# A vision tower on one core: the combine weights stay on chip, the ring of expert weights gets four places, and half of the last residual moves to TensorE

## What is computed

```
h = einsum('bnk,dk->bnd', patches(x), W)                     # 64 x 196 tokens of 192
a = attention(h)       # 12 heads, silu on q, k, v, causal decay instead of a softmax, gate, Wo, layer norm
h = layernorm(h + a)
xn = rms_norm(h); logits = l2(slots) * scale . l2(xn)         # 64 slots
dispatch_w = softmax(logits, over tokens); combine_w = softmax(logits, over slots)
y = einsum('btd,bst->bsd', xn, dispatch_w)                   # the slots' inputs
y = gelu(y @ fc1[s] + b1[s]) @ fc2[s] + b2[s]                # each slot has its own expert: 192 -> 768 -> 192
h = layernorm(h + einsum('bsd,bst->btd', y, combine_w))
```

## Time and profile before

| | us |
|---|---|
| median of three runs | 1286.35 |
| the profiled execution's own time | 1285.4 |
| its span, first to last instruction | 1283.7 |
| TensorE busy with products | 1189.2 (93%) |
| VectorE busy | 816.2 (64%) |
| ScalarE busy | 735.8 (57%) |
| GpSimd busy | 571.7 (45%) |
| granted TensorE clock, mean over the span | 0.957 |

### The profile page before, as it was taken

The page is one execution under the profiler, slowest core; times in us unless marked ns, Lnnn a source line. Parts: engine busy times, 40 slices in busy tenths (PEclk is TensorE's granted clock), DMA queues, the critical chain, the costliest instruction groups (busy, mean ns, idle before and its releaser), DMA issues.

```text
span 1283.7 us, 34970 instructions
## 1 busy us (share of the span) xinstructions
PE 1189.2 (93%) x12938; PEld 956.2 (74%) x12938; DVE 816.2 (64%) x2114; ACT 735.8 (57%) x1677; POOL 571.7 (45%) x878
## 2 busy tenths in 40 slices
PE   5999999999999999999999999999998999997463
PEld 4788888888888888888888888888886555554232
DVE  4677676777777777767777777777673222222797
ACT  5456676776767666777767676666753111110566
POOL 3355455554555554545555455555433000000564
PEclk8999999999999999999999999999999999998555
DMA  4412111111111111111111111121071999994886
GB/s 142 187 49 74 66 53 59 51 50 50 50 50 50 50 66 72 53 54 55 50 50 50 50 50 50 56 81 53 14 265 68 385 419 422 419 393 100 229 261 187
DMA packets 50549, 158.34 MB, mean 123 GB/s; under 512 B 5338, under 2 KB 31312, under 8 KB 38096
## 3 DMA queue, kind: packets, MB, share of 16 engines
q1 hardware_dynamic: 32912, 145.04, 31.0%
q10 hardware_dynamic: 17600, 12.78, 3.2%
HBM read 132.18 MB, written 25.62 MB: 123 GB/s over the span
## 4 chain that ended last, share of the span: by engine, by line
PE 77%; DVE 16%; issue 2%; DMA 1%; ACT 1%; SPq 1%; DVEq 1%; POOL 0%; ACTq 0%; POOLq 0%
PE ps L933 11%; PE ps L934 10%; PE ps L935 10%; DVE p_sb L789 7%; PE ps L993 7%; PE ps L1028 6%; PE ps L1207 5%; PE ps L1224 4%; PE ps L1071 3%; PE ps L976 3%; PE ps L977 3%; PE ps L1011 2%; PE ps L1229 2%; PE ps L1238 2%; DVE res L902 2%; PE ps L1094 2%
## 5 line engine op out<-in xcount | busy, mean ns | idle before, releaser
L412 POOL TENSOR_TENSOR xl<-x_sb,xh 128x392 fp32r<-128x392 f32 x192 | 189.0, 1015 | 86.0 <-DVE gn L764 78.0
L789 DVE TENSOR_TENSOR p_sb<-ps,dec 98x1176 f32<-98x1176 f32 x128 | 176.9, 1382 | 56.0 <-PE ps L993 56.0
L993 PE MATMUL ps<-qm,kT 32*98 32x196 f32 x1536 | 117.0, 343 | 9.6 <-DVE p_sb L789 7.5
L644 ACT ACTIVATE hg<-ps 128x768 f32<-128x768 f32 x32 | 26.0, 812 | 157.2 <-PE ps L1229 157.2
L1028 PE MATMUL ps<-p_sb,vpad 98*32 98x98 f32 x3072 | 112.4, 250 | 1.9 <-DVE p_sb L789 1.9
L1028 PEld LDWEIGHTS ps<-p_sb,vpad 98*32 98x32 f32 x3072 | 84.5, 109 | 35.4 <-issue 24.7
L993 PEld LDWEIGHTS ps<-qm,kT 32*98 32x98 f32 x1536 | 75.2, 158 | 35.1 <-DVE p_sb L789 23.0
L894 DVE COPY y2st<-ps 128x192 f32<-128x192 f32 x32 | 11.4, 358 | 131.4 <-PE ps L1207 131.4
L1253 PE MATMUL ps<-y2b,cbuf 64*98 64x192 f32 x256 | 50.6, 549 | 43.9 <-POOL y2b L512 43.9
L661 ACT ACTIVATE o_sb<-res,nb,rstd 98x192 f32<-98x192 f32 x128 | 59.6, 536 | 51.8 <-DVE nb L917 51.2
L456 POOL TENSOR_TENSOR invn<-nrm,expo 98x4 f32<-98x4 f32 x32 | 32.7, 1021 | 117.7 <-DVE nrm L774 117.4
(11 more groups left out here) (186 smaller groups left out, 3640.9 us busy)
## 6 DMA issues: line engine op xcount, KB each, us to landing
x_sb<-in_xT SPq DMA_DIRECT2D x32, 1176.0 KB, 5.1
w1v<-in_fc SPq DMA_DIRECT2D x32, 1152.0 KB, 7.9
w2v<-in_fc SPq DMA_DIRECT2D x32, 1152.0 KB, 10.5
h_dram<-h SPq DMA_DIRECT2D x32, 294.0 KB
h2r<-h_dram SPq DMA_DIRECT2D x32, 294.0 KB
out<-o_sb ACTq DMA_DIRECT2D x32, 294.0 KB
comb_dram<-cst SPq DMA_DIRECT2D x32, 98.0 KB, 1.7
cbuf<-comb_dram SPq DMA_DIRECT2D x32, 98.0 KB, 3.9
```

Of the source, the lines that this page charges most:

```text
L412: pool.tensor_tensor(xl[:, k], x_sb[:, k], xh[:, k].bitcast(F32), ALU.subtract)\
L789: dve.tensor_tensor(dst, src, rate.unsqueeze(2).to_broadcast([T, PAIRS, 2, TOK]), ALU.mult)\
L993: mm = pe.matmul(ps[0:T, SC_AT + r, mt * TOK:(mt + 1) * TOK].rearrange("p (b n) -> p b n", b=2), kT[rows, g, n], qm[rows, g, :, n], start= ...
```

## The change

- The combine weights of all steps stay on chip in `comb` (25 KB of each partition). Their store, their load and the waits for both are gone.
- The ring of expert weights has four places, all loaded at the end of the first stage. The ring of outputs has four too.
- The two bias products of a pair stand next to each other, ahead of the first products of both halves.
- `y2r` has a place of its own. The rows of pairs 0 to 26 are loaded while the last pairs are computed; only those of pairs 27 to 31 come after the last store. The loads of the first `h2r` stand behind the early rows.
- After the second stage TensorE does 24 products of the identity with itself into a bank that nobody reads.
- In the third stage the residual of tiles 0 and 1 is added by TensorE: a product of the identity and `h2r` starts the bank, the combine products add to it. VectorE adds only tiles 2 and 3, takes the statistics of tiles 0 and 1 from PSUM, does `shift` of the step before, and then the statistics of tiles 2 and 3. ScalarE reads tiles 0 and 1 from PSUM. TensorE's steps of this stage are written out and not in a loop.

```diff
-RING = 6
-TURNS, REST = NU // RING, NU % RING
-assert RING % 2 == 0 and REST % 2 == 0
+RING = 4
...
+U_SOON = 27
+PARTS = ((0, 2 * DEEP), (2 * DEEP, NP))
+Y2 = RING
...
-        slot_at = [region_at + 4 * (2 * F + Y2 * D + n * SLOT) for n in range(EARLY)]
-        place = placer(slot_at[REST])
-        y2r = place("y2r", [128, NP, D])
-        place = placer(slot_at[EARLY - 1] + 4 * SLOT)
-        cbuf, h2r = place("cbuf", [128, DEEP, TOK]), place("h2r", [T, DEEP, 4, D])
-        place = placer(region_at + STAGE_AT)
-        y2b = place("y2b", [128, DEEP, D])
-        res, o_sb = place("res", [T, DEEP, 4, D]), place("o_sb", [T, DEEP, 4, D])
+        y2r, y2b = place("y2r", [128, NP, D]), place("y2b", [128, DEEP, D])
+        comb = place("comb", [128, NP, TOK])
+        place = placer(region_at + 4 * (2 * F + Y2 * D))
+        h2r, res, o_sb = place("h2r", [T, DEEP, 4, D]), place("res", [T, DEEP, 2, D]), place("o_sb", [T, DEEP, 4, D])
...
-            sp.wait_ge(k_mm, 2)
-            for n in range(EARLY, RING):
-                load_weights(n, n)
...
+            def load_y2(u0, u1, p0, p1, there):
+                for a in range(2):
+                    rows = slice(64 * a + 2 * u0, 64 * a + 2 * u1)
+                    sp.dma_start(y2r[rows, p0:p1, :], y2_dram[2 * u0:2 * u1, a, p0:p1, :]).then_inc(there, 16)
+
+            sp.wait_ge(fc2_mm, NU - 4)
+            for m in range(Y2):
+                sp.wait_ge(y2_stored[m], 16 * ((U_SOON - m + Y2 - 1) // Y2))
+            for p in range(0, NP, 2 * DEEP):
+                load_y2(0, U_SOON, p, p + 2 * DEEP, y2r_soon)
+            sp.wait_ge(fc2_mm, NU - 2)
             sp.wait_ge(h2_stored, 16 * NP)
-            sp.wait_ge(comb_stored, 16 * NP)
             for n in range(DEEP):
-                load_comb(n, n)
                 load_h2(n, n)
             for m in range(Y2):
                 sp.wait_ge(y2_stored[m], 16 * ((NU - m + Y2 - 1) // Y2))
             for (p0, p1), there in zip(PARTS, y2r_loaded):
-                for a in range(2):
-                    sp.dma_start(y2r[64 * a:64 * a + 64, p0:p1, :], y2_dram[:, a, p0:p1, :]).then_inc(there, 16)
+                load_y2(U_SOON, NU, p0, p1, there)
             with sp.Fori(0, NP // DEEP - 1) as w:
                 for n in range(DEEP):
                     p = DEEP * w + n
-                    sp.wait_ge(cmb_mm, p + 1)
-                    load_comb(p + DEEP, n)
-                    sp.wait_ge(res_rdy, p + 1)
+                    sp.wait_ge(mv3_rdy, 4 * p + 4)
                     load_h2(p + DEEP, n)
...
+            pool.wait_ge(y2r_soon, 32 * NP // (2 * DEEP))
             pool.wait_ge(y2r_loaded[0], 32)
...
-                    pool.wait_ge(cmb_mm, p + 1)
+                    pool.wait_ge(cmb_mm, 2 * p + 2)
                     bias(p + DEEP, n)
...
-                if d_before:
-                    act.wait_ge(comb_stored, 16 * j)
                 act.wait_ge(cb_mm, j + 1)
-                act.activation(cst[:, :], ps[:, 4, 0:TOK], ACT.Copy).then_inc(cb_sb, 1)
+                act.activation(comb[:, j], ps[:, 4, 0:TOK], ACT.Copy).then_inc(cb_sb, 1)
...
-                    act.activation(o_sb[:, n, t], res[:, n, t], ACT.Identity,
+                    src = ps[0:T, 2 * n, t * D:(t + 1) * D] if t < 2 else res[0:T, n, t - 2]
+                    act.activation(o_sb[:, n, t], src, ACT.Identity,
                                    bias=nb3[:, n, t:t + 1], scale=rstd3[:, n, t:t + 1]).then_inc(o_rdy, 1)
...
-                dve.wait_ge(cmb_mm, p + 1)
+                dve.wait_ge(cmb_mm, 2 * p + 1)
                 dve.wait_ge(h2r_loaded[n], 16 * w + 16)
                 if not at_start(w):
                     dve.wait_ge(o_rdy, 4 * (p + 1 - DEEP))
-                dve.tensor_tensor(res[0:T, n].rearrange("p (x t) d -> p x (t d)", x=2),
-                                  ps[0:T, 2 * n:2 * n + 2, 0:2 * D],
-                                  h2r[:, n].rearrange("p (x t) d -> p x (t d)", x=2), ALU.add)\
-                    .then_inc(res_rdy, 1)
+                dve.tensor_tensor(res[0:T, n].rearrange("p t d -> p (t d)"), ps[0:T, 2 * n + 1, 0:2 * D],
+                                  h2r[:, n, 2:4].rearrange("p t d -> p (t d)"), ALU.add).then_inc(res_rdy, 1)
+                dve.wait_ge(cmb_mm, 2 * p + 2)
+                for t in range(2):
+                    dve.bn_stats(st3[:, n, t, :], ps[0:T, 2 * n, t * D:(t + 1) * D])
+                if not (at_start(w) and n == 0):
+                    shift(p - 1, (n - 1) % DEEP)
                 dve.wait_ge(res_rdy, p + 1)
-                for t in range(4):
-                    dve.bn_stats(st3[:, n, t, :], res[0:T, n, t])
+                for t in range(2):
+                    dve.bn_stats(st3[:, n, 2 + t, :], res[0:T, n, t])
                 dve.drain()
                 for t in range(4):
                     dve.bn_aggr(mv3[:, n, t, :], st3[:, n, t, :]).then_inc(mv3_rdy, 1)
-                if not (at_start(w) and n == 0):
-                    shift(p - 1, (n - 1) % DEEP)
...
                     pe.matmul(ps[:, x, 0:FH], pickb[:, n % 2, x:x + 2].rearrange("p s b -> p (s b)"), bias1[:, f],
                               start=True, stop=False)
+                for x in range(2):
+                    f = slice(x * FH, (x + 1) * FH)
                     for s in range(2):
                         at = 64 * half_of(s, x)
                         pe.matmul(ps[at:at + 64, x, 0:FH], y_u[:, u, s], w1v[n][:, s, f], start=False, stop=False)
...
+            idle_products(6, 24)
             def out_step(p, n, w):
-                pe.wait_ge(cbuf_loaded[n], 16 * w + 16)
-                pe.wait_ge(y2b_rdy, p + 1)
                 if not at_start(w):
                     pe.wait_ge(res_rdy, p + 1 - DEEP)
-                for t in range(4):
+                pe.wait_ge(y2b_rdy, p + 1)
+                for t in (2, 3, 0, 1):
                     a, k = t // 2, t % 2
+                    if t == 0:
+                        if not at_start(w):
+                            pe.wait_ge(o_rdy, 4 * (p + 1 - DEEP))
+                        pe.wait_ge(h2r_loaded[n], 16 * w + 16)
+                        pe.matmul(ps[0:T, 2 * n, 0:2 * D], ident[0:T, 0:T],
+                                  h2r[:, n, 0:2].rearrange("p t d -> p (t d)"), start=True, stop=False)
                     mm = pe.matmul(ps[0:T, 2 * n + a, k * D:(k + 1) * D],
-                                   cbuf[64 * a:64 * a + 64, n, k * T:(k + 1) * T],
-                                   y2b[64 * a:64 * a + 64, n, :], start=True, stop=True)
-                mm.then_inc(cmb_mm, 1)
-            phase3(pe, out_step)
+                                   comb[64 * a:64 * a + 64, p, k * T:(k + 1) * T],
+                                   y2b[64 * a:64 * a + 64, n, :], start=(a == 1), stop=(t != 0))
+                    if k:
+                        mm.then_inc(cmb_mm, 1)
+            for p in range(NP):
+                out_step(p, p % DEEP, p // DEEP)
```

More of the change, by code:

```diff
@@ L266, in phase2 @@
                     step(RING * v + n, n, v)
-            for n in range(REST):
-                step(RING * TURNS + n, n, TURNS)
         def phase3(eng, step):
@@ L334, in _ @@
             store_h2(NP - 4)
-            store_comb(NP - 4)
             store_h2(NP - 3)
```

27 lines of the change are left out of this document (4 added, 23 removed).

## The result

The changed kernel takes 1291.87 us (median of six runs, 1290.67 to 1293.48) against 1286.37 for the kernel before on the same chip: 1.0039 times as long, interval 1.0027 to 1.0051. It is slower by 5.5 us, where 4.7 less had been forecast, and it lies above the top of the range, 1289.

The account below looks back on a forecast made before the run. TensorE was taken to bound the experts' stage, DMA nearly as full, and VectorE most of the third. Gains of 1.6 us (second stage) and 2.6 (third) made 4.2 off 1285.4, 1281.2; 1281.6 was forecast, range 1271 to 1289.

Parts of the forecast that it names:

- part 4: Slots' outputs loaded early, start of third stage: the 11.50 us wait gone, first combine product at T + 6.5.
- T: End of the last expert product, where the third stage starts; 1174.17 us in the kernel before.
- an early load that isn't early: Rival: the early load lands behind the end of stage two; up to 11.5 us back, 1291; chance 0.02.
- Part 1: Combine weights on chip without store or load, and two early weight loads gone: all costed at nothing.
- Part 2: Both bias products first, in the experts' stage: 0.18 us less a pair, bounds 0 and 0.25; 5.67 us a pair.
- The reading of the Trainium skill by which nothing is gained: Rival: the second bias product's weights wait for the first; pair stays 5.853 us, total 1283.5; chance 0.15.
- Part 3: Ring of four, experts' stage: DMA sets 5.81 us a pair, so 1.6 of the 5.6 us gain is kept.
- Part 5: The third stage's new step: 2.94 us against 2.66 before, 2.57 for the last three; TensorE's step 2.1 us.
- the circle: Third stage: `bn_aggr`, GpSimd's `rstd`, `shift` beside `y2b`, two statistics, next `bn_aggr`; 2.94 us a step.

Follow-up runs that it names:

- u24: The changed kernel with the early rows of 24 pairs in place of 27; 1288.39 us, ratio 1.0018 to the kernel before.
- after_nobias: The changed kernel with the two bias products back where they were, each ahead of its half; 1293.75 us, ratio 1.0061 to the kernel before.
- before_bias: The kernel before with the two bias products of a pair next to each other and nothing else; 1274.51 us, ratio 0.9909.
- late_shift: The changed kernel with `shift` of the step before behind `bn_aggr` again; 1282.39 us, ratio 0.9983 to the kernel before.
- bias_split: The kernel before with both bias products together and GpSimd waiting for the third part of the rows only where needed; 1271.23 us, ratio 0.9874.

## Why the prediction was wrong

**The step that failed is part 4**, the first combine product at T + 6.5. It rests on "2.65 MB, 6.3 us at 423 GB/s". The rows moved at 206 GB/s (window 1165 to 1178), 12.9 us for the same bytes, and the 1.2 MB of h2 behind them. Asked for at 1150.60, they began behind the weights asked for before them, ran beside the last of these (which land at 1163.1, with 2.2 us of waiting for TensorE), and so were in flight until after T: the last of them lands at 1179.5, the last of h2 at 1185.1. Two things that I had costed at their old price ran beside them: the last store, which lands at 1179.7, so that the next issue comes at T + 7.6 where it had been T + 2.2, and the small transfer behind it, 6.5 us to the bias add where it had been 4.0. The first product came at 1186.88 = T + 14.7, 8.2 us late.

The other 2.8 us of the missing 11.0 are the first step: 6.29 us from the first product to the end of `bn_aggr`, where I had 3.5. The idle products end 9.2 us before the first combine product, the granted clock falls from 0.91 (1178 to 1184) to 0.50 (1184 to 1190), and at that clock four combine records are 1.52 us and the identity's two 1.53 (1186.88, 1188.40, 1189.93), against the 0.68 and 0.7 of the forecast. In u24, where TensorE stands idle for 0.81 us there and the granted clock is 1.00, the same stretch takes 4.17 us: 2.1 of the 2.8 go with the clock.

The sum: forecast span 1283.7 - 4.2 = 1279.5. Add 11.0 for the start, take 0.4 for a better second stage, add 0.5 for the rest: 1290.6, the span measured. The rival that foresaw this, an early load that isn't early, had two chances in a hundred and nearly the right time, 1291. The time was luck: it priced the rival at the 11.50 us wait coming back (and 1281.6 + 11.5 is 1293), but that wait is gone, and the 11.0 us are the late start and the slow first step. The rival was put aside with "17 us for 9 us of transfers", which counts from the issue, not from when the weights ahead leave the queue, and takes the rate of transfers over 128 partitions for those over 54.

The rate stood in the trace of before. While its rows come in, the window of before shows:

```profile
1182.00:1190.00 8.00, 4.67 (x30) 4.01 (x26) 4.96 (x18) 0.00 (x0) 0.64 (x2) 0.68 1.07 227
```

The 11.50 us wait was that rate, at two transfers of 64 partitions for each part. I read the wait and not its cause. No run here has early rows in transfers over 128 partitions, so what an early load is worth at the full rate is not shown.

**Part 1** (cost of the combine weights on chip: nothing) was not tested alone. What paid for them, the ring of four, was: with it go the two loads at the kernel's start, which part 1 put at nothing too. That holds at the old pace (after_nobias: 189.7 us, as before) and not at the pace of 5.50.

**Part 2** was right in kind and too low in size. A pair with both products together takes 5.50 us (993.94 to 999.45), 0.35 less than 5.853, above my bound of 0.25. The two bias products take 0.53 to the next (993.94 to 994.47) against two times 0.38, 0.23 less; the rest is in the eight records behind them, 1.44 us (994.47 to 995.91) against two times 0.79 (1084.43 to 1085.22 in before), which I hadn't counted. The reading of the Trainium skill by which nothing is gained fell, most plainly in before_bias: T came 11.5 us earlier. TensorE's two loads of bias weights, after:

```profile
993.92 0.30 PEld L1198 LDWEIGHTS ps<-bias,pickb 128*128 128x128 f32 x2
```

Both are done at 994.22, while the first of the two products runs from 993.94, so here the second load lay beside a product that uses the same rows.

**Part 3** was right in kind, and in its sum by luck. The DMA engines set the pace (423 GB/s, share 1.01), TensorE waits for w2 21 times from pair 10 on, and the stage is 1.6 us shorter, as forecast (T came 2.0 us earlier, 0.5 of it an earlier start). But the first pairs took 5.50 us, where I had 5.67, and the last took 7.95 behind the early rows, which the sum didn't have; the two about cancel. What I didn't see is the price: before_bias shows that six places would have kept 11.3.

**Part 5** was right on the circle. `shift` takes 0.546 us in the median (0.55 forecast), `res` comes every 2.94 us on the mean (2.94, 3.27 at each fourth, 2.61 behind it), and VectorE waits for `rstd`. From the first `bn_aggr` to the end it is 97.4 us; the forecast's terms are 90.0 + 6.9 = 96.9. late_shift takes the circle out, for 9.5 us; its stretches at half clock, where TensorE needs 3.07 us a step, part 5 ruled out with "2.1 us even at this slow rate".

## What to carry to other kernels

A transfer's rate depends on whether it covers all 128 partitions: take the rate for an estimate from a transfer of the same shape, and where two transfers each fill half of the partitions look for a layout that lets one fill all. An early load is early only from when the queue ahead of it is empty, and everything small and urgent that is issued later runs beside it. Try each part of a bundle alone: here two moved products gave 11 us, and what they came with took 17 away.

## What the runs showed of the chip

- One transfer over 128 partitions moved 400 to 428 GB/s; over 48, 54, 64 or 96 partitions, 206 to 253, with a DMA share from 0.66 to 1.08. The share tells that engines have work, not how fast it moves.
- Two stores a pair, each to a target in DRAM with a first dimension of 2, held the issuing engine for up to 13.9 us a pair; four, each to 32 rows, cost nothing in that stage.
- Two products in the rounded type next to each other, with a longer run of equal products behind, took 0.35 us less a pair.
- With half of the residual on TensorE, VectorE's steps came every 2.08 us at 2.4 GHz while one of the four places was free, ScalarE's every 2.45, and at 1.2 GHz TensorE made them 3.07. TensorE's clock was 0.50 from 1210 us on in bias_split, whose third stage has no products of the identity; in the changed kernel, which has them, it was 0.50 from 1186 to 1200 and between 0.62 and 1.00 from 1200 to 1280.
